# The first image's front of a non-local attention kernel: x in four loads by halves, scores ahead of the values

## The chip, the cores and the metric

The kernel runs on one core of a Trainium2 chip. The metric is the device time of one launch in microseconds (us). The core's engines are named as in the profile: PE (TensorE, the matmuls; PEld are its weight loads), DVE (VectorE), ACT (ScalarE), POOL (GpSimd) and SP (SyncE, which here only issues transfers). Each runs its own list of instructions in order, and they meet at semaphores.

## The reference

For each of four images x[b] (256 channels by 32 x 32 = 1024 pixels, fp32), with `CQK = 256 // 8 = 32`:

```
q = einsum('oc,bcn->bon', Wq, xf) + bq[None, :, None]      # 32 x 1024
k = einsum('oc,bcn->bon', Wk, xf) + bk[None, :, None]      # 32 x 1024
v = einsum('oc,bcn->bon', Wv, xf) + bv[None, :, None]      # 256 x 1024
scores = einsum('bqi,bqj->bij', q, k)                      # 1024 x 1024
attn = softmax(scores, axis=-1)
out = einsum('bcj,bij->bci', v, attn)
return out.reshape(B, Cc, W, H) + x
```

## The kernel before

Every fp32 operand is split into a high part (rounded to fp32r, names ending in `_hi`) and a low part (what is left, `_lo`), and each product is the sum of three matmuls: high by high, high by low, low by high. Making a high part is called a cut, making a low part a split. Channels lie on the partitions, so x has two tiles of 128 channels (`c` = 0, 1) of 1024 pixels, and most steps work on halves of 512 pixels (`cols(0)`, `cols(1)`).

For each image: project q and k (12 matmuls of 512 columns); project v in eight tiles of 128 pixels (six matmuls of 256 columns each, `v_tile`), which are cut and split in four pairs (`v_split` counts the pairs split); eight score tiles of 128 rows by 1024 columns (`scores`, `first_scores`; two matmuls), of which DVE takes the row maximum (`row_max`) and ACT the sum of the exponentials (`sum_exp`); then the transposed scores (`scores_t`), 16 tiles of 128 x 512, whose exponentials `w_full` are cut and split and multiplied by v (`weigh_v`: four matmuls with the high part, then two with the low part). The list of PE is written out by hand: `turn(b)` weighs image b in 16 steps, and between the steps (`FRONT`) it does the scores and projections of the next image.

The first image has no earlier image to hide behind, and has a front of its own, which the change rewrites:

- SP (line 278) loads the two channel tiles of x, 512 KB each, then the v weights `wv` (256 KB); when these have landed it loads image 1. ACT (line 485) issues the load of the small weights (`small_sb`, 66 KB: the q and k weights and biases).
- PE runs 20 matmuls on zeros (`keep_busy`) until data are there, then `first_project_qk` over the four pieces of x, channel tile by channel tile; so q and k of both halves of the pixels end within the last piece of each half.
- ACT cuts the four pieces of x, then `wv`, then makes k of both halves (`put_k_hi`), the second quarter of q (`put_q_hi`) and the full q of the second half (`put_q2_full`). DVE cuts and splits the q and k weights, splits the pieces of x, makes the first quarter of q itself (line 769), and then the low parts of q and k.
- POOL copies the weights into pairs for the later images (line 418), splits `wv` (line 424), copies two quarters of q (`put_q_dup`), splits the second half of q (`split_q2`: three instructions), then cuts and splits the first three quarters of image 1 and cuts the fourth (`cut_x1`, `split_x1`, lines 408 and 412), and then splits the weights of step 1 (`split_w(1)`, line 402), without which PE can't do the two low matmuls of step 1 (line 1015). So ten instructions lie between `wv`'s split with the q copies, and `split_w(1)`.
- PE then does v tiles 0 and 1, scores 0 to 2, v tiles 2 and 3, scores 3, v tiles 4 and 5, the turning of the four row maxima into rows (`first_rows`), v tile 6, two transposed scores, v tile 7. Step 0 (`first_weigh_v`) has score tile 4 in its middle and score tile 5 behind it, step 1 has score tile 6, and `scores_t(4)` (line 996) opens step 2.

A piece's cut is awaited at `x0_cut`, its split at `x0_split`, q and k of a half at `qk_ready`.

The scores of the first image are put into banks in which q, k and v tiles have stood or will stand: `v_tile(0, 4)` waits for `sum_exp(0, 1)`, `first_scores(3)` for `sum_exp(0, 0)`, and `first_scores(TH)` with TH = 4 for the split of two pairs of v.

Of the kernel before, what the change touches and what calls it, by code (L numbers as in the profile page):

```python
# [6 lines left out]
def nonlocal_attention(nc, x, small, wv_t, out):  # L7
# [52 lines left out]
    with ctx:  # L60
# [3 lines left out]
        def sem(name):  # L64
            return ctx.enter_context(nc.semaphore(name))
# [46 lines left out]
        x0_in = [sem(f"x0_in{c}") for c in range(CT)]  # L112
# [74 lines left out]
        def cols(h):  # L187
            return slice(h * HALF, (h + 1) * HALF)
# [4 lines left out]
        def piece(i):  # L193

            return i // 2, cols(i % 2)
# [4 lines left out]
        def q_home(i):  # L200
            return qk_home(0, i // 2)[2 * CQK:3 * CQK, quarter(i) if i < 2 else cols(0)]
# [34 lines left out]
        def qk_home(b, h):  # L236
            return slot[SLOT[QK, h] if b else h][:, 0:HALF]
# [38 lines left out]
        def _(sp):  # L276
            for c in range(CT):
                sp.dma_start(x_sb[:, 0, c, :], x_v[0, :, c, :]).then_inc(x0_in[c], DMA)
# [82 lines left out]
        def _(pool):  # L361
# [10 lines left out]
            def put_q_dup(i):  # L372
                pool.wait_ge(q_hi_put, i + 1)
                nc.gpsimd.tensor_copy(q_a[0:CQK, Q_PARTS[i]],
                                      q_a[2 * CQK:3 * CQK, Q_PARTS[i]].bitcast(fp32)).then_inc(q_dup_put, 1)
# [38 lines left out]


# [6 lines left out]
            pool.wait_ge(pair_made, 2)  # L422
            pool.wait_ge(wv_cut, 1)
# [3 lines left out]
            put_q_dup(0)  # L427
            pool.wait_ge(q_dup_put, 1)
            put_q_dup(1)
            pool.wait_ge(q_dup_put, 2)  # L430
# [53 lines left out]
        def _(act):  # L484
            act.dma_start(small_sb[:, :], small).then_inc(small_in, DMA)
            act.preload_act_table_set("natural_log_exp_and_others")
            for i in range(4):
                c, part = piece(i)
                act.wait_ge(x0_in[c], DMA)
                nc.scalar.activation(x_hi[:, 0, c, part], x_sb[:, 0, c, part], ACT.Copy).then_inc(x0_cut, 1)  # L490
# [30 lines left out]
            def first_cut_v(i):  # L521
                act.wait_ge(v_ready, i + 1)
                nc.scalar.activation(v_hi[:, 0, VT * i:VT * i + VT, :],
                                     v_home(0, i).rearrange("p (j c) -> p j c", c=C), ACT.Copy).then_inc(v_cut, 1)
# [26 lines left out]
            def put_k_hi(h):  # L551

                act.wait_ge(qk_ready, h + 1)
                nc.scalar.activation(k_a[0:2 * CQK, cols(h)], qk_home(0, h)[0:2 * CQK, :],
                                     ACT.Identity, bias=bias[0:2 * CQK, 0:1]).then_inc(k_hi_put, 1)

            def put_q_hi():

                act.wait_ge(q_lo_put, 1)
                nc.scalar.activation(q_a[2 * CQK:3 * CQK, Q_PARTS[1]], q_home(1),  # L560
                                     ACT.Identity, bias=bias[2 * CQK:3 * CQK, 0:1]).then_inc(q_hi_put, 1)
# [5 lines left out]

            act.wait_ge(wv_in, DMA)
            nc.scalar.activation(wv_hi[:, :, :], wv[:, :, :], ACT.Copy).then_inc(wv_cut, 1)
            act.wait_ge(small_in, DMA)  # L570
            put_k_hi(0)
            put_k_hi(1)
            put_q_hi()
            put_q2_full()
            first_cut_v(0)
            for t in range(TH):
                sum_exp(0, t)
            put_first_rows()
            exp(0)
# [33 lines left out]
        def _(dve):  # L613
# [5 lines left out]
            def twice(w):  # L619
# [5 lines left out]
            dve.wait_ge(wqk_cut, 1)  # L625
            nc.vector.tensor_tensor(twice(wqk_lo), wqk, twice(wqk_hi).bitcast(fp32),
                                    ALU.subtract).then_inc(wqk_split, 1)

            for i in range(4):
                c, part = piece(i)  # L630
                dve.wait_ge(x0_cut, i + 1)
                nc.vector.tensor_tensor(x_lo[:, 0, c, part], x_sb[:, 0, c, part],  # L632
                                        x_hi[:, 0, c, part].bitcast(fp32), ALU.subtract).then_inc(x0_split, 1)
# [117 lines left out]
            def finish(b, h, c):  # L751
# [9 lines left out]
                if (b, h) == (0, 0):  # L761
# [6 lines left out]
            dve.wait_ge(qk_ready, 1)  # L768
            nc.vector.tensor_scalar(out=q_a[2 * CQK:3 * CQK, Q_PARTS[0]], in0=q_home(0),
                                    scalar1=bias[2 * CQK:3 * CQK, 0:1], scalar2=None,  # L770
                                    op0=ALU.add).then_inc(q_hi_put, 1)
            put_q_lo(0)
            put_k_lo(0)
# [5 lines left out]
            split_v(0, 0)  # L779
            first_cut_v(1)  # L780
            split_v(0, 1)
            invert_sums()
            first_cut_v(2)
# [62 lines left out]
        def _(pe):  # L846
# [23 lines left out]
            def first_project_qk(i):  # L870
                c, part = piece(i)
                dst = qk_home(0, i % 2)
                if i == 0:
                    pe.wait_ge(wqk_cut, 1)
                pe.wait_ge(x0_cut, i + 1)
                nc.tensor.matmul(dst, wqk_hi[:, c, :], x_hi[:, 0, c, part], start=(c == 0), stop=False)
                if i == 0:
                    pe.wait_ge(wqk_split, 1)
                nc.tensor.matmul(dst, wqk_lo[:, c, :], x_hi[:, 0, c, part], start=False, stop=False)
                pe.wait_ge(x0_split, i + 1)  # L880
                last = nc.tensor.matmul(dst, wqk_hi[:, c, :], x_lo[:, 0, c, part], start=False, stop=(c == CT - 1))  # L881
                if c == CT - 1:
                    last.then_inc(qk_ready, 1)
# [55 lines left out]
            def v_tile(b, t):  # L939
                px = slice(t * P, (t + 1) * P)  # L940
                dst = v_home(b, t // VT)[:, t % VT * C:(t % VT + 1) * C]
                terms = [(xs[:, b % 2, c, px], w[:, c, :]) for c in range(CT)
                         for xs, w in ((x_hi, wv_hi), (x_hi, wv_lo), (x_lo, wv_hi))]
                if b == 0 and t == 0:

                    for c in range(CT):
                        for xs in (x_hi, x_lo):
                            nc.tensor.matmul(dst, xs[:, 0, c, px], wv_hi[:, c, :],
                                             start=(c == 0 and xs is x_hi), stop=False)
                    pe.wait_ge(wv_split, 1)  # L950
                    for c in range(CT):
                        nc.tensor.matmul(dst, x_hi[:, 0, c, px], wv_lo[:, c, :], start=False, stop=(c == CT - 1))
                    return
                last = group(dst, terms)
                if t % VT == VT - 1:
                    last.then_inc(v_ready, 1)

# [41 lines left out]
            def weigh_ready(b, h, j):  # L999
                if h == 0 and j % VT == 0:  # L1000
                    pe.wait_ge(v_split, 4 * b + 1 + j // VT)
                wait_w_cut(pe, PER * b + JT * h + j)
# [76 lines left out]
            keep_busy(20, QUARTER)  # L1079
            for i in range(4):  # L1080
                first_project_qk(i)
            pe.wait_ge(wv_cut, 1)
            v_tile(0, 0)
            v_tile(0, 1)
            first_scores(0)
            first_scores(1)
            first_scores(2)

            pe.wait_ge(q2_full_put, 1)
            v_tile(0, 2)  # L1090
            v_tile(0, 3)
            first_scores(3)
# [71 lines left out]
```

## Time and profile before

| | us |
|---|---|
| median of 3 runs | 164.04 (163.82 to 164.06) |
| the profiled execution, its own time | 163.81 |
| its span, first to last instruction | 162.0 |
| PE busy in the span | 157.5 (97%) |
| DVE busy | 133.9 (83%) |
| ACT busy | 109.2 (67%) |
| POOL busy | 60.0 (37%) |

Busy time counts an instruction from its start to its end, and matmuls overlap in the pipeline, so the end of one and the start of the next are read from the starts. A row of the timeline can hold several instructions in a row (x2, x4); its duration is then that of all of them.

### The profile page before, as it was taken

The numbers are of one execution on the slowest core, as the hardware profiler recorded it, in microseconds if no ns is written. First come the engines' busy times: TensorE is split into PE (matmuls) and PEld (weight loads), VectorE is DVE, ScalarE is ACT, GpSimd is POOL, SyncE is SP. The second block draws the span as 40 slices with busy tenths as digits, with TensorE's granted clock in tenths as the row PEclk, the third lists the DMA queues.
The fourth block names the chain that finished last, engine by engine and source line by source line (L and its number), as shares of the span: only waits on it lengthen the run. The fifth ranks groups of instructions, "written<-read, shape, count | busy, mean of one in ns | idle before, by whom it ended". The sixth has DMA issues, their size and how long they took to land.

```text
span 162.0 us, 2456 instructions
## 1 busy us (share of the span) xinstructions
PE 157.5 (97%) x788; PEld 132.3 (82%) x788; DVE 133.9 (83%) x215; ACT 109.2 (67%) x200; POOL 60.0 (37%) x68
## 2 busy tenths in 40 slices
PE   7999999999999999999999999999999999999993
PEld 5677887798888887798888897788888898888882
DVE  1899998888988989997989989895989779846952
ACT  3679887969999545827999646736896655756400
POOL 4479946256222316348443300342333300124500
PEclk9999999999999999999999999999999999999999
DMA  4576672152103030162711130162320330003003
GB/s 161 187 299 166 243 235 89 31 151 63 55 0 97 1 129 2 37 144 67 268 39 49 54 129 0 37 146 67 121 61 1 97 129 0 0 5 129 0 0 130
DMA packets 7780, 14.67 MB, mean 91 GB/s; under 512 B 1504, under 2 KB 2072, under 8 KB 7768
## 3 DMA queue, kind: packets, MB, share of 16 engines
q1 hardware_dynamic: 6728, 13.46, 25.4%
q0 software_dynamic: 608, 0.80, 2.2%
q10 hardware_dynamic: 432, 0.26, 0.5%
q8 instruction: 6, 0.10, 0.3%
q14 instruction: 6, 0.05, 0.1%
HBM read 4.79 MB, written 4.20 MB: 55 GB/s over the span
## 4 chain that ended last, share of the span: by engine, by line
PE 90%; DMA 2%; ACT 2%; DVE 2%; issue 1%; DVEq 0%
PE acc L1009 32%; PE acc L1015 16%; PE slot L849 11%; PE st L996 9%; PE slot L909 7%; PE slot L1009 5%; DMA small_sb<-small 2%; PE slot L1015 2%; ACT dump L504 2%; PE slot L861 2%; PE slot L866 2%; PE slot L935 1%; DVE negmax L667 1%; PE slot L881 1%; DVE x_lo L632 0%
## 5 line engine op out<-in xcount | busy, mean ns | idle before, releaser
L402 POOL TENSOR_TENSOR w_lo<-w_full,w_hi 128x512 fp32r<-128x512 f32 x21 | 28.0, 1338 | 46.6 <-ACT w_full L542 25.4
L1009 PE MATMUL acc<-w_hi,v_hi 128*128 128x512 f32 x112 | 44.3, 395 | 0.0
L1009 PE MATMUL acc<-w_hi,v_lo 128*128 128x512 f32 x112 | 44.1, 394 | 0.0
L542 ACT ACTIVATE w_full<-st 128x512 f32<-128x512 f32 x62 | 36.8, 594 | 7.6 <-PE st L996 7.5
L504 ACT ACTIVATE dump<-slot,negmax 128x1024 f32<-128x1024 f32 x29 | 32.5, 1119 | 10.5 <-DVE negmax L667 10.1
L667 DVE TENSOR_REDUCE negmax<-slot 128x1 f32<-128x1024 f32 x29 | 35.2, 1217 | 2.7 <-PE slot L909 2.7
L1015 PE MATMUL acc<-w_lo,v_hi 128*128 128x512 f32 x112 | 37.4, 396 | 0.0
L734 DVE TENSOR_TENSOR w_lo<-w_full,w_hi 128x512 fp32r<-128x512 f32 x43 | 30.7, 719 | 3.6 <-issue 0.5
L1009 PEld LDWEIGHTS acc<-w_hi,v_hi 128*128 128x128 f32 x112 | 21.1, 189 | 5.0 <-issue 0.2
L1009 PEld LDWEIGHTS acc<-w_hi,v_lo 128*128 128x128 f32 x112 | 21.2, 189 | 4.8
L1015 PEld LDWEIGHTS acc<-w_lo,v_hi 128*128 128x128 f32 x112 | 21.0, 188 | 4.8
L996 PE MATMUL st<-q_b,k_b 98*128 98x512 f32 x62 | 24.5, 398 | 0.1
L725 DVE CAST w_hi<-w_full 128x512 fp32r<-128x512 f32 x40 | 19.5, 489 | 3.0 <-ACT w_full L542 1.5
L539 ACT ACTIVATE w_hi<-st 128x512 fp32r<-128x512 f32 x24 | 14.3, 594 | 6.2 <-PE st L996 6.0
L849 PE MATMUL slot<-wv_hi,x_hi 128*128 128x256 f32 x62 | 17.4, 281 | 0.4 <-ACT dump L504 0.4
L849 PE MATMUL slot<-wv_lo,x_hi 128*128 128x256 f32 x62 | 17.4, 281 | 0.0
L849 PE MATMUL slot<-wv_hi,x_lo 128*128 128x256 f32 x62 | 17.3, 280 | 0.0
L909 PE MATMUL slot<-k_a,q_a 96*128 96x512 f32 x48 | 15.2, 397 | 0.0
L531 ACT ACTIVATE v_hi<-slot 128x512 fp32r<-128x512 f32 x12 | 7.2, 599 | 11.8 <-PE slot L849 11.8
L265 POOL DMA_DIRECT2D q_b<-shift_rows x7 | 4.2, 602 | 29.5 <-DVE shift_rows L706 27.0
L715 DVE TENSOR_TENSOR v_lo<-slot,v_hi 128x512 fp32r<-128x512 f32 x16 | 11.0, 690 | 3.8 <-ACT v_hi L531 3.7
L909 PEld LDWEIGHTS slot<-k_a,q_a 96*128 96x128 f32 x48 | 13.0, 310 | 1.1
(102 smaller groups left out, 225.2 us busy)
## 6 DMA issues: line engine op xcount, KB each, us to landing
out<-x_sb SPq DMA_DIRECT2D x7, 512.0 KB, 2.8
x_sb<-x SPq DMA_DIRECT2D x3, 1024.0 KB, 5.1
k_b<-k_a SPq DMA_DIRECT2D x8, 192.0 KB, 2.6
q_b<-q_a SPq DMA_DIRECT2D x8, 192.0 KB, 2.6
x_sb<-x SPq DMA_DIRECT2D x2, 512.0 KB, 4.2
k_a<-qk_parts SPq DMA_DIRECT2D x12, 64.0 KB, 2.0
q_a<-qk_parts SPq DMA_DIRECT2D x12, 64.0 KB, 2.2
k_a<-qk_parts POOLq DMA_DIRECT2D x6, 64.0 KB, 2.2
```

The lines of the kernel that those rows point to most:

```text
L402: nc.gpsimd.tensor_tensor(w_lo[:, r, :], w_full[:, r, :], w_hi[:, r, :].bitcast(fp32), ALU.subtract).then_inc(w_split_pool, 1)
L504: nc.scalar.activation(dump[:, t % 2, :], s_home(b, t), ACT.Exp, bias=negmax[:, t:t + 1], accum_out=rowsum[:, t:t + 1]).then_inc(rowsum_re ...
L539: nc.scalar.activation(w_hi[:, r, :], st_home(n), ACT.Exp).then_inc(w_cut_act, 1)
L542: nc.scalar.activation(w_full[:, r, :], st_home(n), ACT.Exp).then_inc(exp_done, 1)
L667: nc.vector.tensor_reduce(out=negmax[:, t:t + 1], in_=s_home(b, t), op=ALU.max, axis=AX.X, negate=True).then_inc(negmax_ready, 1)
L725: nc.vector.tensor_copy(w_hi[:, r, :], w_full[:, r, :]).then_inc(w_cut_dve, 1)
L734: nc.vector.tensor_tensor(w_lo[:, r, :], w_full[:, r, :], w_hi[:, r, :].bitcast(fp32), ALU.subtract).then_inc(w_split_dve, 1)
L849: last = nc.tensor.matmul(dst, lhs, rhs, start=(i == 0), stop=(i == len(terms) - 1))
L909: last = nc.tensor.matmul(s_home(b, t)[:, cols(h)], pixels(b, t), k_a[0:K_A, cols(h)], start=True, stop=True)
L996: nc.tensor.matmul(st_home(n), k_b[0:K_B, j * P:(j + 1) * P], q_b[0:K_B, cols(h)], start=True, stop=True).then_inc(st_ready, 1)
L1009: nc.tensor.matmul(dst, v[:, b % 2, j, c * P:(c + 1) * P], w_hi[:, n % RING, part], start=(j == 0 and v is v_hi), stop=False)
L1015: return nc.tensor.matmul(dst, v_hi[:, b % 2, j, c * P:(c + 1) * P], w_lo[:, n % RING, part], start=False, stop=(j == JT - 1))
```

## The change

It loads the first image's x in four pieces of 256 KB, both channel tiles of the first half of the pixels first, all from SP, with the small weights (now from SP too) behind the first piece. A piece `i` is now channel tile `i % 2` of half `i // 2`, so q and k of the first half are complete after two pieces. On DVE the first piece's split goes ahead of the split of the q and k weights. ACT makes k and q of the first half, then k and q of the second, then cuts `wv`; DVE no longer makes q's first quarter. POOL copies q's first quarter ahead of the weight pairs, its second behind them, and splits `wv` after that. PE runs 16 zero matmuls ahead of the projection and four behind it, and the v tiles come behind the scores; the cut of the first pair of v moves behind ACT's sums, its split on DVE behind the second pair's, and the wait counts follow.

```
@@ SP
-            for c in range(CT):
-                sp.dma_start(x_sb[:, 0, c, :], x_v[0, :, c, :]).then_inc(x0_in[c], DMA)
+            for i in range(4):
+                c, part = piece(i)
+                sp.dma_start(x_sb[:, 0, c, part], x_v[0, :, c, part]).then_inc(x0_in[i], DMA)
+                if i == 0:
+                    sp.dma_start(small_sb[:, :], small).then_inc(small_in, DMA)
             sp.dma_start(wv[:, :, :], wv_t).then_inc(wv_in, DMA)
...
-            return i // 2, cols(i % 2)
+            return i % CT, cols(i // CT)
...
@@ POOL
+            put_q_dup(0)
+            pool.wait_ge(q_dup_put, 1)
             for half, (parts, made) in enumerate(((wqk_hi, wqk_cut), (wqk_lo, wqk_split))):
...
             pool.wait_ge(pair_made, 2)
+            put_q_dup(1)
+            pool.wait_ge(q_dup_put, 2)
             pool.wait_ge(wv_cut, 1)
             nc.gpsimd.tensor_tensor(wv_lo[:, :, :], wv[:, :, :], wv_hi[:, :, :].bitcast(fp32),
...
-            put_q_dup(0)
-            pool.wait_ge(q_dup_put, 1)
-            put_q_dup(1)
-            pool.wait_ge(q_dup_put, 2)
             split_q2()
...
@@ ACT
-            act.dma_start(small_sb[:, :], small).then_inc(small_in, DMA)
...
+            act.wait_ge(small_in, DMA)
+            put_k_hi(0)
+            put_q_hi(0)
+            put_k_hi(1)
+            put_q_hi(1)
             act.wait_ge(wv_in, DMA)
             nc.scalar.activation(wv_hi[:, :, :], wv[:, :, :], ACT.Copy).then_inc(wv_cut, 1)
-            act.wait_ge(small_in, DMA)
-            put_k_hi(0)
-            put_k_hi(1)
-            put_q_hi()
             put_q2_full()
-            first_cut_v(0)
             for t in range(TH):
                 sum_exp(0, t)
             put_first_rows()
+            first_cut_v(0)
             exp(0)
...
@@ DVE
-            dve.wait_ge(wqk_cut, 1)
-            nc.vector.tensor_tensor(twice(wqk_lo), wqk, twice(wqk_hi).bitcast(fp32),
-                                    ALU.subtract).then_inc(wqk_split, 1)
             for i in range(4):
                 c, part = piece(i)
+                if i == 1:
+                    dve.wait_ge(wqk_cut, 1)
+                    nc.vector.tensor_tensor(twice(wqk_lo), wqk, twice(wqk_hi).bitcast(fp32),
+                                            ALU.subtract).then_inc(wqk_split, 1)
...
-            nc.vector.tensor_scalar(out=q_a[2 * CQK:3 * CQK, Q_PARTS[0]], in0=q_home(0),
-                                    scalar1=bias[2 * CQK:3 * CQK, 0:1], scalar2=None,
-                                    op0=ALU.add).then_inc(q_hi_put, 1)
+            put_k_lo(0)
             put_q_lo(0)
-            put_k_lo(0)
...
-            split_v(0, 0)
             first_cut_v(1)
             split_v(0, 1)
+            first_cut_v(2)
+            split_v(0, 0)
             invert_sums()
-            first_cut_v(2)
             split_v(0, 2)
...
@@ PE
+            def first_project_qk(i, w, xs):
+                c, part = piece(i)
+                return nc.tensor.matmul(qk_home(0, i // CT), w[:, c, :], xs[:, 0, c, part],
+                                        start=(c == 0 and w is wqk_hi and xs is x_hi),
+                                        stop=(c == CT - 1 and xs is x_lo))
+
+            def first_project_all():
+                pe.wait_ge(wqk_cut, 1)
+                pe.wait_ge(x0_cut, 1)
+                first_project_qk(0, wqk_hi, x_hi)
+                pe.wait_ge(x0_split, 1)
+                first_project_qk(0, wqk_hi, x_lo)
+                pe.wait_ge(x0_cut, 2)
+                first_project_qk(1, wqk_hi, x_hi)
+                pe.wait_ge(wqk_split, 1)
+                first_project_qk(0, wqk_lo, x_hi)
+                first_project_qk(1, wqk_lo, x_hi)
+                pe.wait_ge(x0_split, 2)
+                first_project_qk(1, wqk_hi, x_lo).then_inc(qk_ready, 1)
+                for i in (2, 3):
+                    pe.wait_ge(x0_cut, i + 1)
+                    first_project_qk(i, wqk_hi, x_hi)
+                    first_project_qk(i, wqk_lo, x_hi)
+                    pe.wait_ge(x0_split, i + 1)
+                    last = first_project_qk(i, wqk_hi, x_lo)
+                last.then_inc(qk_ready, 1)
...
+            def first_v_high():
+                pe.wait_ge(wv_cut, 1)
+                for c in range(CT):
+                    for xs in (x_hi, x_lo):
+                        nc.tensor.matmul(v_home(0, 0)[:, 0:C], xs[:, 0, c, 0:P], wv_hi[:, c, :],
+                                         start=(c == 0 and xs is x_hi), stop=False)
+
+            def first_v_low():
+                pe.wait_ge(wv_split, 1)
+                for c in range(CT):
+                    nc.tensor.matmul(v_home(0, 0)[:, 0:C], x_hi[:, 0, c, 0:P], wv_lo[:, c, :],
+                                     start=False, stop=(c == CT - 1))
...
-                    pe.wait_ge(v_split, 4 * b + 1 + j // VT)
+                    pe.wait_ge(v_split, 4 * b + 1 + j // VT if b + j else 2)
...
-            keep_busy(20, QUARTER)
-            for i in range(4):
-                first_project_qk(i)
-            pe.wait_ge(wv_cut, 1)
-            v_tile(0, 0)
-            v_tile(0, 1)
+            keep_busy(16, QUARTER)
+            first_project_all()
+            keep_busy(4, QUARTER)
             first_scores(0)
+            first_v_high()
             first_scores(1)
             first_scores(2)
+            first_v_low()
+            v_tile(0, 1)
             pe.wait_ge(q2_full_put, 1)
             v_tile(0, 2)
+            first_scores(3)
             v_tile(0, 3)
-            first_scores(3)
```

## Rows read from the trace of the kernel before

**Rows 1.** Busy us by stage (windows): stretch, length, PE, PEld, DVE, ACT, POOL, clock, DMA.

```profile
24.00:156.00 132.00, 132.00 (x651) 111.96 (x650) 113.00 (x181) 91.74 (x171) 43.92 (x44) 1.00 0.22 68
```

**Rows 2.** Timeline of PE: start us, us, engine, line, operation, tiles, count, [idle before].

```profile
1.06 4.45 PE L1076 MATMUL st<-idle 128*128 128x256 bf16 x20 [1.06 <-DVE idle L614]
5.27 0.59 PE L876 MATMUL slot<-x_hi,wqk_hi 128*128 128x512 f32 x1
...
8.18 0.39 PE L879 MATMUL slot<-x_hi,wqk_lo 128*128 128x512 f32 x1
8.41 0.39 PE L881 MATMUL slot<-x_lo,wqk_hi 128*128 128x512 f32 x1
...
13.69 0.74 PE L935 MATMUL acc<-k_a,q_a 96*128 96x512 f32 x2
...
22.79 0.63 PE L1015 MATMUL acc<-w_lo,v_hi 128*128 128x512 f32 x2
...
23.93 0.39 PE L996 MATMUL st<-q_b,k_b 98*128 98x512 f32 x1
```

**Rows 3.** Timeline of POOL.

```profile
5.56 0.75 POOL L418 CAST wqk_pair<-wqk_lo 128x128 fp32r<-128x128 f32 x1
7.64 1.58 POOL L424 TENSOR_TENSOR wv_lo<-wv,wv_hi 128x512 fp32r<-128x512 f32 x1 [1.34 <-ACT wv_hi L569]
...
10.72 0.61 POOL L380 CAST q_a<-qk_rest 32x512 fp32r<-32x512 f32 x1 [0.18 <-ACT qk_rest L565]
...
18.23 1.29 POOL L412 TENSOR_TENSOR x_lo<-x_sb,x_hi 128x512 fp32r<-128x512 f32 x1
19.59 1.10 POOL L408 CAST x_hi<-x_sb 128x512 fp32r<-128x512 f32 x1
20.92 1.29 POOL L402 TENSOR_TENSOR w_lo<-w_full,w_hi 128x512 fp32r<-128x512 f32 x1 [0.23 <-ACT w_full L542]
```

**Rows 4.** Timeline of SP's queue, the transfers that it issues.

```profile
0.74 0.86 SPq L278 DMA_DIRECT2D x_sb<-x  x2
...
6.45 0.39 SPq L282 DMA_DIRECT2D x_sb<-x  x1
```

**Rows 5.** Windows of the first loads; last columns: DMA share and GB/s.

```profile
1.75:2.75 1.00, 1.00 (x7) 0.69 (x6) 0.00 (x0) 0.71 (x1) 0.94 (x2) 1.00 0.62 133
2.75:4.10 1.35, 1.35 (x8) 0.98 (x7) 0.00 (x0) 0.00 (x0) 0.09 (x1) 1.00 1.04 401
...
5.25:5.75 0.50, 0.50 (x4) 0.45 (x2) 0.50 (x2) 0.40 (x1) 0.50 (x2) 1.00 1.02 397
```

**Rows 6.** Timeline of ACT.

```profile
4.50 1.15 ACT L490 ACTIVATE x_hi<-x_sb 128x512 fp32r<-128x512 f32 x2 [2.04 <-DMA x_sb<-x]
...
6.88 0.62 ACT L569 ACTIVATE wv_hi<-wv 128x512 fp32r<-128x512 f32 x1
8.21 1.31 ACT L554 ACTIVATE k_a<-slot,small_sb 64x512 fp32r<-64x512 f32 x2 [0.72 <-PE slot L881]
9.55 0.47 ACT L560 ACTIVATE q_a<-slot,small_sb 32x256 fp32r<-32x256 f32 x1
```

**Rows 7.** Timeline of DVE.

```profile
4.71 0.29 DVE L624 CAST wqk_hi<-small_sb 128x256 fp32r<-128x256 f32 x1 [3.43 <-DMA small_sb<-small]
...
5.38 2.68 DVE L632 TENSOR_TENSOR x_lo<-x_sb,x_hi 128x512 fp32r<-128x512 f32 x4
...
14.57 1.22 DVE L667 TENSOR_REDUCE negmax<-acc 128x1 f32<-128x1024 f32 x1
...
19.53 0.68 DVE L734 TENSOR_TENSOR w_lo<-w_full,w_hi 128x512 fp32r<-128x512 f32 x1
```

**Rows 8.** Chain that ended last, in order of time: start us, us, what.

```profile
18.42 0.71 PE slot L849 x6
```

**Rows 9.** Timeline of POOL and of DVE, 48 to 51 us.

```profile
48.43 1.30 POOL L402 TENSOR_TENSOR w_lo<-w_full,w_hi 128x512 fp32r<-128x512 f32 x1 [2.96 <-issue]
49.34 0.93 DVE L734 TENSOR_TENSOR w_lo<-w_full,w_hi 128x512 fp32r<-128x512 f32 x1
```

More of the change, by code:

```diff
@@ L110, in nonlocal_attention @@
         slot = [ctx.enter_context(nc.psum_tensor(f"slot{i}", [P, N], fp32)) for i in range(2)]
-        x0_in = [sem(f"x0_in{c}") for c in range(CT)]
+        x0_in = [sem(f"x0_in{i}") for i in range(4)]
         x1_in = sem("x1_in")
@@ L488, in _ @@
                 c, part = piece(i)
-                act.wait_ge(x0_in[c], DMA)
+                act.wait_ge(x0_in[i], DMA)
                 nc.scalar.activation(x_hi[:, 0, c, part], x_sb[:, 0, c, part], ACT.Copy).then_inc(x0_cut, 1)
@@ L555, in put_k_hi, with put_q_hi @@
                                      ACT.Identity, bias=bias[0:2 * CQK, 0:1]).then_inc(k_hi_put, 1)
-            def put_q_hi():
-                act.wait_ge(q_lo_put, 1)
-                nc.scalar.activation(q_a[2 * CQK:3 * CQK, Q_PARTS[1]], q_home(1),
+            def put_q_hi(i):
+                if i:
+                    act.wait_ge(q_lo_put, i)
+                nc.scalar.activation(q_a[2 * CQK:3 * CQK, Q_PARTS[i]], q_home(i),
                                      ACT.Identity, bias=bias[2 * CQK:3 * CQK, 0:1]).then_inc(q_hi_put, 1)
@@ L766, in finish @@
                                                scalar=bv_sb[:, c:c + 1], in1=x_sb[:, b, c, cols(h)], op0=ALU.add, op1=ALU.add).then_inc(acc_read, 1)
-            dve.wait_ge(qk_ready, 1)
-            nc.vector.tensor_scalar(out=q_a[2 * CQK:3 * CQK, Q_PARTS[0]], in0=q_home(0),
-                                    scalar1=bias[2 * CQK:3 * CQK, 0:1], scalar2=None,
-                                    op0=ALU.add).then_inc(q_hi_put, 1)
+            put_k_lo(0)
             put_q_lo(0)
-            put_k_lo(0)
             put_k_lo(1)
@@ L868, in project_qk @@
                 both_halves(CT - 1).then_inc(qk_ready, 1)
-            def first_project_qk(i):
+            def first_project_qk(i, w, xs):
                 c, part = piece(i)
[L872 to L883, printed above, removed]
+                return nc.tensor.matmul(qk_home(0, i // CT), w[:, c, :], xs[:, 0, c, part],
[21 more added lines that the diff above has]
+                last.then_inc(qk_ready, 1)
             def pixels(b, t):
@@ L943, in v_tile @@
                          for xs, w in ((x_hi, wv_hi), (x_hi, wv_lo), (x_lo, wv_hi))]
[L944 to L953, printed above, removed]
                 last = group(dst, terms)
```

## The prediction

> **What bounds the kernel now.** I read the table of busy time by stage first. From 24 to 156 us PE is busy for 132.00 of 132.00 us [rows 1]. So nothing behind 24 us can be won by ordering, and whatever the change gains is the shift of the moment at which PE takes up that unbroken run. I measure it at `scores_t(4)`, line 996, which starts at 23.93 [rows 2]. Before that point the reader looks, engine by engine in the timeline, for what releases PE last. The last place where it can be held is step 1: its two low matmuls, line 1015, start at 22.79 [rows 2] and need `split_w(1)` of POOL, which ran from 20.92 to 22.21 [rows 3]: 0.58 us to spare. Behind them come two matmuls of score tile 6; a matmul of 512 columns takes 0.23 (8.18 to 8.41), so 22.79 + 4 x 0.23 = 23.72, and the 0.21 up to 23.93 is a wait, for the sums of tile 4.
>
> POOL matters because it has no slack of its own: from `split_q2` at 10.72 to the cut that ends at 20.69 its ten instructions follow one another [rows 3]. It then waited 0.2 for its operand. Whatever shifts 10.72 shifts all of it.
>
> A difference of 0.2%, 0.33 us, is about what a measurement of this kernel tells from no change.
>
> **Loads.** Before, two loads of 512 KB were issued in 0.86 us from 0.74 on [rows 4], the small one from ACT at the same time. 133 GB/s moved up to 2.75, 401 behind [rows 5]. Both (592 KB) were through at 2.75 + (592 - 133) / 401 = 3.89; ACT started on x at 4.50 [rows 6], 0.61 later, DVE on the weights at 4.71 [rows 7], 0.82 later. After, 262 KB end at 2.75 + 129 / 401 = 3.07 and the small load, 68 KB, at 3.24. With the same lags ACT starts at 3.68 and DVE at 4.06. The bounds: the small load lags no more than x did (3.85), or nothing is won (4.71). I take 4.06, since the order in the queue is what the change turns. SP issues three loads more, at 0.43 each 1.3 us; this hides behind the transfers, of which each piece needs 0.65 at 401 GB/s. `wv` has the same bytes ahead of it, so it still lands at about 6.45, when image 1 is issued [rows 4], and ACT asks for it later than that.
>
> A page of the Trainium skill speaks against the cutting: "DMA: Bandwidth & Descriptors", section "Rules for kernel authors", wants 1 MiB or more in a transfer. Here the 256 KB of `wv` moved at 397 GB/s [rows 5] beside 401 in the window before, so by the row the four pieces cost nothing; by the rule the pieces would land later than I say, which is the fourth rival below.
>
> **Projection.** DVE's chain of weight cut, weight split and four splits of x took 4.71 to 8.06 [rows 7], 3.35 us; with the same instructions it ends at 4.06 + 3.35 = 7.41. PE: twenty matmuls of 256 columns on zeros took 4.45, one starting every 0.21 [rows 2], which is the 1.2 GHz level (the clock column shows 1.00 throughout, and doesn't tell it); 512 columns in 0.23 are 2.4 GHz. Sixteen end at 1.06 + 16 x 0.21 = 4.47. The first piece is cut at 3.68 + 0.62 = 4.30, so PE goes on without a gap: high by high 4.47, high by low behind the first split (4.39 + 0.7) at 5.1, both at the low level, until 5.53. With the clock up at about 5.5 as before (the matmul at 5.27 took 0.59, later ones 0.39), ten are left: the last starts at 5.53 + 9 x 0.23 = 7.63 and ends at 8.02. Before, the last ended at 8.41 + 0.39 = 8.80. So q and k are whole 0.78 earlier.
>
> **The cut of wv, and what hangs on it.** It was done at 6.88 + 0.62 = 7.50 [rows 6], ahead of k. Now it stands behind k and q of both halves: k of half 1 starts at 8.02 + 0.1 (before, half 0 ended at 8.41 - 3 x 0.23 + 0.39 = 8.11 and ACT began at 8.21), the step to the next is 0.63 (two took 1.31, one of them 0.68), q 0.45, the cut 0.62: done at 9.80. POOL follows 0.14 later as before (7.50 to 7.64) and needs 1.29, as its other subtractions of this size do, or 1.58 as it took before beside DVE's splits [rows 3]; at 9.9 DVE reads PSUM, so I take 1.29: `wv_lo` ends at E = 11.23 (to 11.52). The weight pairs (0.75 the longer) fit between the two q copies, since POOL has until 9.94; without that cover they would add to E. `split_q2` follows at E + 0.07 = 11.30, against 10.72: POOL is **0.58 later** (to 0.87).
>
> **PE's side.** Behind E stand two low matmuls of v tile 0 and tiles 1 and 2, 14 matmuls at 0.117 (six in 0.71 [rows 8]): score tile 3 starts at 11.23 + 0.06 + 1.64 = 12.93 and is whole 0.7 later (two in 0.74 [rows 2]); the fourth row maximum starts at 13.65, against 14.57 [rows 7]: **0.92 earlier**. What follows it (row maxima to rows, exponentials, the first weighing) has the same instructions on its path; ACT's added cut of v pair 0 fits into its wait for the transposed scores. DVE's three earlier row maxima start from about 10.0 and don't hold it. PE would reach line 1015 at 22.79 - 0.92 = 21.87.
>
> **The sum.** POOL doesn't let it. Its cut chain ends 0.58 later: `split_w(1)` runs from 20.76 + 0.58 = 21.34 to 22.63, PE starts its low matmuls at 22.69, four matmuls later stands at 23.62, against 23.93: -0.31. (The wait for the sums of tile 4 is gone, they come 0.9 earlier.) With 1.58 for `wv_lo` it is -0.02; with 3.85 for DVE's start little more, since PE's zero matmuls end at 4.47 anyhow. Later consumers have room: image 1 is split by POOL's last piece at 28 us plus the same 0.6, and image 2's load goes out 0.6 later, for work far behind. Against its own execution that is 163.81 - 0.31 = 163.50; that execution lies 0.23 under the median, so I say 164.04 - 0.31 = **163.7** for the median. Its own range is 163.4 to 164.0, from POOL's instructions each stretched or shortened by a collision.
>
> **Rivals.**
> 1. *POOL gains back what it lost.* Before, its cut at 19.59 took 1.10 instead of 0.61 (10.72), because DVE's `split_w(0)` had started at 19.53 [rows 3, 7]. If DVE meets a gap or waits itself, POOL has 0.49 less: -0.8, 163.2. For it: the two move apart by 1.5 us. Against: POOL has no gap there, so they meet again.
> 2. *DVE loses the meeting, and it gets slower.* At 49.34 DVE's split started while POOL's (48.43 to 49.73) ran, and ended at 50.27, 0.54 behind it [rows 9]: the one that came second waited whole. `split_w(0)` asks at 19.53 - 0.92 = 18.61. POOL's subtraction of 18.23 then stands at 18.81 to 20.10. If DVE comes 0.2 later than I think, it waits for 20.10 and ends at 20.64, against 20.21; its row maximum of tile 4, the sums and score tile 6 follow as much later: +0.43, 164.5. It decides at 18.81. The Trainium skill has this as a rule ("SBUF — State Buffer", section "Who interferes with whom": GpSimd and a VectorE instruction with two SBUF inputs exclude each other for a whole instruction, and the one that issues first wins); the rows agree.
> 3. *The clock stays low.* Between 4.9 and 5.1 PE now idles, and it waits for pieces. If the low level lasts through the projection, ten matmuls cost 0.2 more each: E comes 2 us later, +1.7, 165.7. For it: before, PE had no gap from 1.06 to the rise. Against: the gap is 0.2 us.
> 4. *The loads win nothing.* Then DVE starts at 4.71 as before and its chain ends at 8.06, PE at 8.5 instead of 8.02: E + 0.47, +0.16, 164.2. Against it: the bytes ahead of the first piece are halved.
>
> **Chances.** Forecast 0.52, half of it beyond -0.33; rival 1 0.15, rival 2 0.15, rival 3 0.08, rival 4 0.10. Faster 0.26 + 0.15 = 0.41; within 0.2% 0.26 + 0.10 = 0.36; slower 0.23. The range goes from 163.0, a little under rival 1, to 164.8, above rival 2; it leaves out rival 3 and little else.
>
> **What would show it.** First x cut at about 3.7 and weight cut at 4.1; the last projection matmul ending near 8.0; `wv_hi` done at 9.8; `wv_lo` ending near 11.2; the fourth row maximum at 13.7; `split_w(1)` ending at 22.6 and PE's low matmuls of step 1 idle before it by about 0.8. I am wrong if PE is not held by POOL there, if projection matmuls start 0.43 apart behind 6 us, or if `split_w(0)` takes over 1 us.

## The result, and the profile after

After takes **165.82 us** (165.12 to 166.88) against 163.96 (163.8 to 164.2) on the same chip: ratio 1.0116 [1.0083, 1.0150], **slower by 1.2%**. I had said 163.7, with 163.0 to 164.8 as the range. The profiled execution of after took 165.12 (span 163.3), the lowest of the timed ones; that of before 163.81 (span 162.0).

**Where the loss stands.** Stage windows and PE's timeline:

```profile
24.00:156.00 132.00, 132.00 (x649) 111.85 (x649) 113.51 (x182) 93.03 (x174) 43.91 (x44) 1.00 0.23 73
```

```profile
6.12 0.50 PE L872 MATMUL slot<-x_hi,wqk_hi 128*128 128x512 f32 x1 [0.70 <-ACT x_hi L492]
...
8.35 0.42 PE L872 MATMUL slot<-x_lo,wqk_hi 128*128 128x512 f32 x1
...
13.91 0.62 PE L947 MATMUL acc<-k_a,q_a 96*128 96x512 f32 x2
...
21.58 0.73 PE L1031 MATMUL acc<-w_lo,v_hi 128*128 128x512 f32 x2 [0.27 <-DVE w_lo L738]
...
24.06 0.63 PE L1031 MATMUL acc<-w_lo,v_hi 128*128 128x512 f32 x2
...
25.25 0.40 PE L1011 MATMUL st<-q_b,k_b 98*128 98x512 f32 x1
```

PE is again unbroken from 24 to 156 [rows 1], and `scores_t(4)` starts at 25.25 instead of 23.93 [rows 2]: 1.32 later, which is the difference of the executions (165.12 - 163.81 = 1.31). The place that I measured at was right, and the sign was wrong. (The median is 0.7 above this execution; what adds that is shown by the experiments.) The last projection matmul starts at 8.35 against 8.41, and score tile 3 at 13.91 against 13.69 [rows 2], so the front won nothing. The fourth row maximum starts at 14.58 against 14.57; in this execution the loss arises behind it.

**What holds PE there.** The chain that ended last, in order of time (start us, us, what):

```profile
10.33 0.50 PE acc L947
...
14.58 1.24 DVE negmax L671
...
15.91 0.98 DVE shift_parts L678
...
20.26 1.27 DVE w_lo L738
...
21.58 0.73 PE acc L1031 x2
```

It runs over DVE and not over POOL. DVE's timeline and POOL's:

```profile
6.10 2.12 DVE L636 TENSOR_TENSOR x_lo<-x_sb,x_hi 128x512 fp32r<-128x512 f32 x3 [0.90 <-ACT x_hi L492]
...
14.58 1.23 DVE L671 TENSOR_REDUCE negmax<-acc 128x1 f32<-128x1024 f32 x1 [0.22 <-PE acc L947]
15.91 0.97 DVE L678 CAST shift_parts<-negmax 128x4 fp32r<-128x4 f32 x1
...
20.18 1.35 DVE L738 TENSOR_TENSOR w_lo<-w_full,w_hi 128x512 fp32r<-128x512 f32 x1
```

```profile
10.81 1.29 POOL L431 TENSOR_TENSOR wv_lo<-wv,wv_hi 128x512 fp32r<-128x512 f32 x1 [0.28 <-ACT wv_hi L577]
12.16 0.61 POOL L383 CAST q_a<-qk_rest 32x512 fp32r<-32x512 f32 x1
...
15.57 1.29 POOL L415 TENSOR_TENSOR x_lo<-x_sb,x_hi 128x512 fp32r<-128x512 f32 x1
...
19.69 1.28 POOL L415 TENSOR_TENSOR x_lo<-x_sb,x_hi 128x512 fp32r<-128x512 f32 x1
...
22.08 1.30 POOL L405 TENSOR_TENSOR w_lo<-w_full,w_hi 128x512 fp32r<-128x512 f32 x1
```

Before, in the timelines of both engines, the same cast of four columns fell into the end of another instruction of POOL, a cut up to 16.08, and the small subtraction behind the cast was 0.02 ahead of POOL's next subtraction:

```profile
15.47 0.61 POOL L408 CAST x_hi<-x_sb 128x512 fp32r<-128x512 f32 x1
15.90 0.20 DVE L674 CAST shift_parts<-negmax 128x4 fp32r<-128x4 f32 x1
16.14 0.17 DVE L676 TENSOR_TENSOR shift_parts<-negmax,shift_parts 128x4 fp32r<-128x4 f32 x1
16.16 1.31 POOL L412 TENSOR_TENSOR x_lo<-x_sb,x_hi 128x512 fp32r<-128x512 f32 x1
```

DVE arrives there at the same time in both kernels (15.90, 15.91). POOL's chain of cuts and subtractions is 12.16 - 10.72 = 1.44 later [rows 3], so another of its instructions stands there: a subtraction from 15.57 to 16.86, and the cast ends at 16.88. It costs 0.97 - 0.20 = 0.77. Before, the good meeting was luck, by 0.02 us. `split_w(0)` starts at 20.18, inside the subtraction of 19.69 to 20.97, and ends 0.56 behind it: 1.35 against 0.68 [rows 7], 0.67 more. The two make 0.77 + 0.67 = 1.44 (the same figure as POOL's shift by chance), of which 0.13 is won back between them. The second ends at 21.53, 1.32 behind 19.53 + 0.68 = 20.21, and PE waits for it. `split_w(1)`, which I had taken for the bound, ends at 23.38, ahead of PE's low matmuls at 24.06.

**Loads.** SP's queue, ACT's timeline and the windows (last columns: DMA share, GB/s):

```profile
1.19 0.42 SPq L281 DMA_DIRECT2D small_sb<-small  x1
1.65 1.38 SPq L279 DMA_DIRECT2D x_sb<-x  x3
```

```profile
3.50 0.63 ACT L492 ACTIVATE x_hi<-x_sb 128x512 fp32r<-128x512 f32 x1 [1.47 <-DMA x_sb<-x]
5.44 2.05 ACT L492 ACTIVATE x_hi<-x_sb 128x512 fp32r<-128x512 f32 x3 [1.30 <-DMA x_sb<-x]
10.03 0.63 ACT L577 ACTIVATE wv_hi<-wv 128x512 fp32r<-128x512 f32 x1
```

```profile
1.75:2.75 1.00, 1.00 (x7) 0.69 (x6) 0.00 (x0) 0.28 (x1) 0.94 (x2) 1.00 0.85 280
2.75:4.10 1.35, 1.35 (x8) 0.98 (x7) 0.29 (x1) 0.60 (x1) 0.09 (x1) 1.00 0.88 225
4.10:5.25 1.15, 1.15 (x5) 0.59 (x3) 1.03 (x2) 0.03 (x1) 0.00 (x0) 1.00 0.88 292
```

The first piece is cut at 3.50, before the 4.50 of [rows 6]. Up to 2.75 more moves than before (280 GB/s against 133). But behind it, where 401 GB/s moved [rows 5], it is 225 and 292, the second piece is cut at 5.44 only, and DVE (0.90) and PE (0.70) wait.

### The profile page after: what moved, and what is told of

Its sections match the earlier page's. It is cut to its first block, busy times and chain, and to the rows that moved or that the text cites. A ratio compares the mean times of both kernels' runs of the same rounds, so it can differ in the third digit from the quotient of the medians.

```text
span 163.3 us, 2458 instructions
## 1 busy us (share of the span) xinstructions
PE 157.3 (96%) x788; PEld 131.7 (81%) x788; DVE 135.1 (83%) x214; ACT 110.1 (67%) x201; POOL 59.0 (36%) x68
## 4 chain that ended last, share of the span: by engine, by line
PE 88%; DVE 7%; DMA 2%; SPq 0%; issue 0%; ACT 0%; DVEq 0%
PE acc L1025 31%; PE acc L1031 16%; PE slot L849 11%; PE st L1011 9%; PE slot L921 7%; PE slot L1025 5%; PE slot L1031 2%; DMA x_sb<-x 2%; PE slot L861 2%; PE slot L866 2%; PE slot L947 1%; DVE x_lo L636 1%; DVE v_lo L719 1%; DVE k_a L646 1%; DVE w_lo L738 1%; DVE negmax L671 1%
## 5 line engine op out<-in xcount | busy, mean ns | idle before, releaser
L738 DVE TENSOR_TENSOR w_lo<-w_full,w_hi 128x512 fp32r<-128x512 f32 x43 | 31.4, 734 | 3.3
```

What stands on the lines that cost most here:

```text
L738: nc.vector.tensor_tensor(w_lo[:, r, :], w_full[:, r, :], w_hi[:, r, :].bitcast(fp32), ALU.subtract).then_inc(w_split_dve, 1)
```

## The experiments

**A** is the meetings of DVE with POOL's subtractions, **B** the loads: they land late and differently each time. In its first form B blames the small load in SP's queue, in its second the halves (rows of 2 KB instead of 4).

**after_again**: after, unchanged.

> The changed kernel once more, for a second profile. Theory A (DVE waits for POOL): in its first profile DVE's first shift cast took 0.97 us instead of 0.20 and split_w(0) 1.35 instead of 0.68, together 1.44 us, about the whole of the 1.3 by which that execution was longer; a second profile shows the same two, within 0.3. Theory B (loads): the loads by halves move at 225 to 307 GB/s instead of 400, the second piece is there at 5.4 instead of my 4.3, and as this differs from execution to execution it makes the spread of 1.8 us; the second profile has the second piece elsewhere (4.5 to 6.5) and its length moves with it.

165.78 (165.56 to 166.41), ratio 1.0128 [1.0104, 1.0152]; profiled execution 165.70. Its timelines of ACT and DVE:

```profile
6.78 1.28 ACT L492 ACTIVATE x_hi<-x_sb 128x512 fp32r<-128x512 f32 x2 [1.01 <-DMA x_sb<-x]
...
16.47 0.99 DVE L678 CAST shift_parts<-negmax 128x4 fp32r<-128x4 f32 x1
...
20.77 1.35 DVE L738 TENSOR_TENSOR w_lo<-w_full,w_hi 128x512 fp32r<-128x512 f32 x1
```

Both meetings stand though everything is 0.6 later: POOL hangs on the same late loads, so the two keep their phase. Here the second piece is cut at 5.14, the third at 6.78 only. Both causes are seen.

**loads_only** (of before: the four half loads and the small one behind the first, nothing else) and **order_only** (of after: the loads of before).

```
loads_only, in before:
-            for c in range(CT):
-                sp.dma_start(x_sb[:, 0, c, :], x_v[0, :, c, :]).then_inc(x0_in[c], DMA)
+            for i in range(4):
+                c, part = piece(i)
+                sp.dma_start(x_sb[:, 0, c, part], x_v[0, :, c, part]).then_inc(x0_in[i], DMA)
+                if i == 0:
+                    sp.dma_start(small_sb[:, :], small).then_inc(small_in, DMA)
...
-            act.dma_start(small_sb[:, :], small).then_inc(small_in, DMA)
...
order_only, in after: the same lines the other way round
```

> The kernel before with the loads alone changed: four by halves from SP, the small one behind the first, in the order of the change; everything else as before. Theory A expects no change beyond 0.3 us, since the order of POOL and DVE is that of before. Theory B expects the last pieces later than the 5.8 of before (6 to 6.5), the last projection matmul later by as much, so 0.3 to 0.8 us more, and a spread over 0.8 us.

> The changed kernel with the loads of before: two of 512 KB from SP, the small one from ACT. Theory A expects the two long DVE instructions to stay, and 165.0 to 165.5. Theory B expects the spread to fall to that of before (0.4 us), the second piece at 5.85 as before, and the time near the lower end of the changed kernel's, 165.1 or less.

loads_only: 165.14 (165.1 to 165.21), 1.0079 [1.0064, 1.0094]. order_only: 166.77 (165.52 to 166.92), 1.0162 [1.0125, 1.0199]; three of its four executions take 166.7 to 166.9, one 165.52. Both halves of the change lose by themselves, and each loses more than either theory had put down (0.8 at most for loads_only, 165.5 at most for order_only). loads_only, timelines of POOL and DVE:

```profile
16.30 1.27 POOL L415 TENSOR_TENSOR x_lo<-x_sb,x_hi 128x512 fp32r<-128x512 f32 x1
...
14.93 1.22 DVE L669 TENSOR_REDUCE negmax<-acc 128x1 f32<-128x1024 f32 x1
...
16.46 1.13 DVE L678 TENSOR_TENSOR shift_parts<-negmax,shift_parts 128x4 fp32r<-128x4 f32 x1
```

DVE is 14.93 - 14.57 = 0.36 later, and that is enough: its subtraction of the shift, 0.02 ahead of POOL's before, now starts inside POOL's and takes 1.13 instead of 0.17. 0.36 + 0.96 = 1.32, the measured 1.3. So A needs no new order, only a change of phase. order_only, PE's timeline:

```profile
5.34 0.77 PE L870 MATMUL slot<-x_hi,wqk_hi 128*128 128x512 f32 x1 [0.69 <-ACT x_hi L490]
...
8.86 0.63 PE L870 MATMUL slot<-x_hi,wqk_lo 128*128 128x512 f32 x1
9.29 0.54 PE L870 MATMUL slot<-x_lo,wqk_hi 128*128 128x512 f32 x1
```

With x at the old time, PE's sixteen zero matmuls end 0.69 too early, and the projection's start 0.43 apart, the 1.2 GHz step, until 9.3: the low clock of my third rival.

**order_busy20**: order_only with twenty zero matmuls.

```
-            keep_busy(16, QUARTER)
+            keep_busy(20, QUARTER)
```

> The run with the loads of before and the order of the change (166.77, projection matmuls 0.43 apart up to 9.3 us), with twenty zero matmuls ahead of the projection again instead of sixteen. Theory C (the gap between the zero matmuls and the first piece, 4.7 to 5.3, kept TensorE at its low level) expects matmuls 0.23 apart behind about 6.5 us, 1.2 to 1.6 us less (165.2 to 165.6) and a spread under 0.4. Rival: the order of the projection with its waits keeps the clock low by itself; then 166.5 or more.

165.50 (165.41 to 165.56), 1.0100 [1.0086, 1.0114]: 1.27 less than order_only. Its timeline of PE, where the step is 0.23 from the second row on:

```profile
1.06 3.70 PE L1090 MATMUL st<-idle 128*128 128x256 bf16 x20 [1.06 <-DVE idle L616]
...
7.52 0.40 PE L870 MATMUL slot<-x_hi,wqk_hi 128*128 128x512 f32 x1
7.75 0.40 PE L870 MATMUL slot<-x_hi,wqk_lo 128*128 128x512 f32 x1
```

So the low clock is what cost order_only that. That the gap kept it low isn't shown. Twenty zero matmuls took 3.70, where order_only's sixteen took 3.60: the last six start 0.11 apart, the 2.4 GHz step, from 3.94 on, ahead of the four that were added and at a time when order_only still went at 0.21; and 0.47 without work follows them here too. Only the times speak for the four: all of order_busy20's executions lie at 165.4 to 165.6, one in four of order_only's. Cast (0.97) and `split_w(0)` (1.35) stay, and with them the loss.

**small_act**: after, the small load from ACT again. **whole_sp**: before, the small load on SP behind the first 512 KB. **small_first**: before, on SP ahead of x.

```
small_act, in after:
-                if i == 0:
-                    sp.dma_start(small_sb[:, :], small).then_inc(small_in, DMA)
...
+            act.dma_start(small_sb[:, :], small).then_inc(small_in, DMA)
whole_sp, in before (small_first: the SP line ahead of the loop):
+                if c == 0:
+                    sp.dma_start(small_sb[:, :], small).then_inc(small_in, DMA)
...
-            act.dma_start(small_sb[:, :], small).then_inc(small_in, DMA)
```

> The changed kernel with the small load from ACT again, x still in four loads from SP. If it is the small load's place in SP's queue that holds the second piece, this lands at 4.3 to 4.7 and the time falls by 0.5 to 0.9 us (theory B, first form). If it is the halves themselves that are slow (second form), the second piece stays at 5.2 or later and the time stays within 0.4 of the changed kernel's. Theory A expects no change but that of chance meetings.

> The kernel before with one edit: the small load issued by SP behind the first 512 KB of x, not by ACT. If the small load's place in SP's queue slows what is behind it (form 1), the windows behind 2.75 us move less than 320 GB/s and the second tile of x lands at 6.3 or later, with a spread over 0.5 us. If it is the halves (form 2), the windows stay near 400 GB/s; the small load then lands about 0.2 later than before and the time stays within 0.4 of before.

> The kernel before with the small load ahead of x in SP's queue. The weights are cut at about 3.6 instead of 4.71, and DVE has their split behind it when x comes, so its chain ends up to 0.4 earlier. As POOL's chain hangs on the same projection, both shift together: 163.4 to 163.8, if x isn't later by as much. If the small load slows what is behind it, x lands later and the time is 164.0 or more.

small_act: 165.17 (165.11 to 165.23), 1.0081 [1.0066, 1.0096], 0.65 less than after and without its spread. The difference is one of medians: the profiled executions of the two take 165.13 and 165.12, after's being its fastest. whole_sp: 164.64 (164.43 to 165.88), 1.0059 [1.0036, 1.0082]. small_first: 163.73 (163.59 to 165.07), 1.0001 [0.9986, 1.0017]. Windows of small_act, and behind them of whole_sp, of a later stretch:

```profile
1.75:2.75 1.00, 1.00 (x7) 0.67 (x6) 0.00 (x0) 0.71 (x1) 0.94 (x2) 1.00 0.66 171
2.75:4.10 1.35, 1.35 (x8) 0.95 (x7) 0.04 (x1) 0.21 (x1) 0.09 (x1) 1.00 1.07 362
4.10:5.25 1.15, 1.14 (x4) 0.36 (x2) 0.96 (x3) 1.01 (x2) 0.00 (x0) 1.00 0.92 306
```

```profile
5.25:5.75 0.50, 0.50 (x4) 0.40 (x3) 0.50 (x2) 0.00 (x0) 0.48 (x1) 1.00 0.63 225
...
6.25:6.75 0.50, 0.50 (x3) 0.40 (x2) 0.03 (x1) 0.00 (x0) 0.00 (x0) 1.00 0.20 78
```

Halves without the small load among them move at 362 and 306, where after has 225 and 292; but after is ahead by then (280 against 171), and summed over 1.75 to 5.25 the two have moved 1012 and 920 KB, before 1143.

The other traces put most of this on the halves. The six kernels with halves and the small load from ACT (small_act, clear_small, mend1 to mend4) moved 917 to 1012 KB in that stretch, the four with it behind the first piece (after, after_again, loads_only, clear_after) 833 to 920, those with whole tiles and it from ACT (before, order_only, order_busy20, clear_before) 1130 to 1144. small_act is the best of its six: in clear_small, with the same loads, the third piece comes late as well; timeline of ACT:

```profile
6.39 1.29 ACT L495 ACTIVATE x_hi<-x_sb 128x512 fp32r<-128x512 f32 x2 [0.87 <-DMA x_sb<-x]
```

Whole tiles with the small load among them trail off: in before the loads fill the DMA engines up to 5.75 [rows 5] and are through; in whole_sp the share falls from 0.63 to 0.20, and ACT cuts the second tile at 7.12 instead of 5.82 (timelines of both). This is whole_sp's slowest execution, 165.88, the others take 164.4 to 164.8; and in it DVE's subtraction of the shift waits for POOL (1.28), so a meeting is part of its loss. Cut or whole, the kernels with the small load in SP's queue behind the first piece are the slower ones, B's first form; in what the queue moves, the second form holds too. The issue of the small load itself puts the next piece 0.46 later (1.65 instead of 1.19 in SP's queue above), and how much of the 0.65 that is, no run separates.

In small_act three pieces are cut without a gap from 3.89 on, yet its projection ends no earlier; timeline of PE:

```profile
5.89 0.63 PE L871 MATMUL slot<-x_hi,wqk_hi 128*128 128x512 f32 x1
6.32 0.85 PE L871 MATMUL slot<-x_hi,wqk_lo 128*128 128x512 f32 x2
...
8.39 0.39 PE L871 MATMUL slot<-x_lo,wqk_hi 128*128 128x512 f32 x1
```

From 5.89 to 6.32 is 0.43, the low level, and so is the step inside the pair at 6.32; the step is 0.23 from 7.00 on, before from 6.55. Earlier data was worked on at the lower clock.

**clear_after** and **clear_before**: POOL's subtractions of image 1's first three quarters cut to one column, in after and in before (the rest of that low part is left out). **clear_small**: clear_after with small_act's load.

```
+            nc.gpsimd.memset(x_lo[:, 1, :, 0:3 * QUARTER].bitcast(fp32), 0.0).then_inc(x1_zero, 1)
...
-                nc.gpsimd.tensor_tensor(x_lo[:, 1, :, quarter(i)], x_sb[:, 1, :, quarter(i)],
-                                        x_hi[:, 1, :, quarter(i)].bitcast(fp32), ALU.subtract).then_inc(x1_split, 1)
+                part = quarter(i) if i == 3 else slice(i * QUARTER, i * QUARTER + 1)
+                nc.gpsimd.tensor_tensor(x_lo[:, 1, :, part], x_sb[:, 1, :, part],
+                                        x_hi[:, 1, :, part].bitcast(fp32), ALU.subtract).then_inc(x1_split, 1)
```

> The changed kernel with POOL's three subtractions for the low part of image 1's first three quarters cut to one column each (the rest is set to zero early, so that low part is left out). DVE then meets no POOL instruction of 1.3 us. Theory A (DVE waits for POOL) expects the first shift cast at 0.2 instead of 0.97, split_w(0) at 0.7 instead of 1.35, and 1.2 to 1.5 us less than the changed kernel: 164.0 to 164.5. Theory B (the loads are the loss) expects 165.3 or more, since the loads stay.

> The same cut in the kernel before, as control. There the shift cast takes 0.20 and split_w(0) 0.68 already, so theory A expects 163.6 to 163.9, no change; if POOL's load as such slowed PE or DVE (rival), this would gain as much as clear_after, over 1 us.

> Both suspected costs taken away from the changed kernel: the small load from ACT, and POOL's three subtractions for image 1 cut to one column each (that low part is left out). If the two are the whole loss and add up, 165.8 - 0.6 - 1.35 = 163.85, within 0.3 of the kernel before. If something else of the change costs too, it stays above 164.2; if the front had a gain hidden behind the two, it comes out under 163.5.

clear_after: 164.44 (163.83 to 165.6), 1.0040 [1.0021, 1.0060], 1.38 less than after. clear_before: 163.80 (163.66 to 163.93), 0.9993 [0.9984, 1.0002]: the cut alone gives nothing. clear_small: 163.86 (163.6 to 164.2), 0.9999 [0.9990, 1.0008]. Timeline of DVE in clear_after:

```profile
16.24 0.56 DVE L682 CAST shift_parts<-negmax 128x4 fp32r<-128x4 f32 x1
...
20.09 0.68 DVE L742 TENSOR_TENSOR w_lo<-w_full,w_hi 128x512 fp32r<-128x512 f32 x1
```

The cast still waits for POOL's cut there (0.56), `split_w(0)` for nothing. So the meetings cost after 1.38 and the small load's place 0.65 (165.82 - 165.17), 2.03 together; after is 1.86 over before in its own comparison, 1.96 (165.78 - 163.82) in that of after_again, and with both away the change neither gains nor loses. Each costs about as much with the other away: 1.31 (165.17 - 163.86) and 0.58 (164.44 - 163.86). Taken alone, after against small_act isn't clear of after's spread; after_again (0.61) and the 0.58 are. The two causes account for the whole loss.

**mend1 to mend4**: small_act with POOL's work put elsewhere, to miss the meetings and keep the computation whole.

```
mend1, POOL's order as it is then (other waits left out):
             cut_x1(0)
             pool.wait_ge(shift_ready, 1)
             split_x1(0)
...
             cut_x1(1)
             pool.wait_ge(w_split_dve, SPLIT_COUNT[0])
             cut_x1(2)
             split_w(1)
             split_x1(1)
             split_w(3)
             split_x1(2)
             cut_x1(3)
             split_x1(3)
mend2: also PE's first_scores(3) ahead of v_tile(0, 2)
mend3: mend2; POOL has split_x1(1) ahead of cut_x1(2), without the wait for
       step 0's split, and split_x1(2), cut_x1(3) ahead of split_w(3)
mend4: mend3; DVE has split_v(0, 2) ahead of split_v(0, 0), and the wait
       counts follow
```

> Whole computation: the changed kernel with the small load from ACT, and POOL's work for image 1 put where DVE doesn't need the way: it waits for the shifts before its first subtraction, for split_w(0) before its third cut, does split_w(1) then, and the rest of image 1 after it. Theory A expects both long DVE instructions gone and 1.2 to 1.4 us less than with the small load from ACT alone (165.17): 163.7 to 164.0, level with the kernel before. Theory B expects 165.0.

> mend1 with score tile 3 ahead of v tile 2, so that the fourth row maximum needn't wait for it (0.20 to 0.28 us idle before it in the changed kernel). Theory A: another 0.2 to 0.3 less, 163.4 to 163.7, faster than the kernel before by 0.2 to 0.5. Rival: the fourth row maximum starts 0.3 earlier, but PE then waits for split_w(1) of POOL, and nothing is won over mend1.

> mend2 with another order on POOL: it waits for the shifts before its first subtraction, splits two quarters of image 1 and cuts the third, does split_w(1), then the third subtraction and the fourth cut, and only the last subtraction behind split_w(3), as in the kernel before. Theory A (what counts is which DVE instruction meets which POOL instruction) expects the shift cast and sub at 0.2 each, split_w(0) at no more than 0.9, no DVE instruction over 1.2 us up to 32 us, and 163.5 to 164.0. If what mend1 lost late came not from the moved subtractions but from the front itself, it stays at 164.8.

> mend3, whole computation, with DVE's split of v pair 0 behind that of pair 2, since in mend3 DVE stood idle 0.57 us for ACT's moved cut of that pair. If that idle time is what mend3 still lost, split_w(0) starts at about 19.3 instead of 19.78 and the time is 163.8 to 164.0, level with the kernel before; if not, it stays at 164.3.

mend1: 164.80 (164.63 to 165.16), 1.0057 [1.0044, 1.0069]. mend2: 165.09 (164.89 to 165.29), 1.0072 [1.0059, 1.0084]. mend3: 164.34 (164.25 to 164.4), 1.0031 [1.0019, 1.0044]. mend4: 164.23 (163.66 to 164.48), 1.0018 [1.0007, 1.0028]. All four missed the time that I expected; mend4 came out where I had put it if DVE's idle time was not what mend3 lost (164.3). mend1 misses the early meetings: `scores_t(4)` at 24.02, 0.09 behind before. But the moved subtractions meet DVE later; timelines of DVE and POOL:

```profile
26.54 1.60 DVE L738 TENSOR_TENSOR w_lo<-w_full,w_hi 128x512 fp32r<-128x512 f32 x1
...
26.12 1.47 POOL L413 TENSOR_TENSOR x_lo<-x_sb,x_hi 128x512 fp32r<-128x512 f32 x1
```

In mend2 and mend3 DVE idles 0.54 and 0.57 for ACT's cut of v pair 0, which the change had put behind the sums. In mend4 that wait is gone, and `split_w(0)` comes at 19.62, 0.03 behind POOL's cut of 19.59; timelines of DVE and POOL:

```profile
19.62 1.12 DVE L736 TENSOR_TENSOR w_lo<-w_full,w_hi 128x512 fp32r<-128x512 f32 x1 [0.20 <-ACT w_full L542]
...
19.59 0.61 POOL L409 CAST x_hi<-x_sb 128x512 fp32r<-128x512 f32 x1
```

By their medians, none of the four beats before.

## Why the prediction was wrong, point by point

- **Where to measure** was right: PE unbroken behind 24, and `scores_t(4)` gives the whole difference.
- **Loads** failed behind the first piece. First piece 3.50 (I said 3.68) and weights 3.68 (4.06) were near. I had 133 GB/s up to 2.75 and 401 behind it; it was 280, then 225 and 292. `wv` was there a microsecond later than I said (image 1 is issued at 7.48, not at 6.45), which cost nothing, since ACT asked for it at 10.03. The Trainium skill, "DMA: Bandwidth & Descriptors", section "Rules for kernel authors", had spoken against cutting x; in what was moved the traces agree (917 to 1012 KB with halves, 1130 to 1144 with whole tiles), and my "by the row the four pieces cost nothing" was wrong. In the time the cutting isn't seen, for clear_small has the halves and takes what before takes; what the median loses is 0.65, by the small load's place. The same page, section "Issuing engines are not separate DMA queues", says that another issuing engine saves only the time of issuing; small_act and after, which differ in that alone, differ by 0.65, of which issuing can be 0.46; what is left over isn't clear of the spread, so these runs don't contradict the page. Whether the queue does more stays open: the traces show the rates, not why.
- **Projection.** I had the last matmul start at 7.63. It was 8.35: the second piece was late. Without that lateness (small_act) it was 8.39, because the low clock lasted longer than to my 5.5. Both eat the 0.78 that I had counted; rivals 3 and 4, each in part. That rival 3's time, 165.7, lies near the measured 165.82 is chance: in after's profile the step is 0.23 from 6.45 on, and the loss came by another way. (Two sums were off by a little, 1.06 + 16 x 0.21 is 4.42 and not 4.47, 5.53 + 9 x 0.23 is 7.60; neither matters here.)
- **The cut of wv** was mis-sized by the same: 10.66 instead of 9.80, and `wv_lo` ends at 12.10 instead of 11.23.
- **PE's side** failed in "0.92 earlier": the fourth row maximum starts at 14.58, before 14.57. 0.72 of the 0.93 missing came with the projection (8.35 instead of 7.63). The rest is a path: I let all of it hang on `wv_lo`, but the chain goes through DVE's low parts of k, which I didn't walk: the second matmul of the first score, at 10.33, waits for `put_k_lo(1)`. PE's low matmuls of v tile 0 start at 12.22, 0.12 behind `wv_lo`, when score tile 2 is issued.
- **"What follows it has the same instructions on its path"** is the step that gave the wrong sign. From the fourth row maximum to the end of `split_w(0)` it took 20.21 - 14.57 = 5.64 before and 21.53 - 14.58 = 6.95 after: the same instructions, two of them held by POOL. With the row maximum 0.01 later, that is the whole 1.32 of the profiled executions. I had put one of the two down as rival 2, at 0.15 and +0.43; it took 0.67. I had looked at DVE's wide subtractions only, and not seen the cast of four columns, whose wait costs as much.
- **"POOL doesn't let it"**: POOL was 1.44 later, not 0.58, but not the bound: `split_w(1)` ended at 23.38, ahead of the matmuls that need it. What its shift did was to turn its phase against DVE's.

Two of my three signs of being wrong came: PE was not held by POOL there, and `split_w(0)` took over 1 us.

Shown by experiments: the meetings (clear_after against clear_before), and that the small load's place costs time (clear_small against clear_after, small_act against after_again). Not shown: what in SP's queue makes the loads late, and what decided in order_only and order_busy20 when the clock rose. Only read from timelines: why mend1 to mend4 don't reach before.

## What to carry to other kernels

Where GpSimd and VectorE both work from SBUF on a chain without slack, lay their timelines over each other before and after every shift, small instructions included: in loads_only a shift of 0.36 us cost 1.3. When a chain is moved, forecast the phase of the two chains, and not only their lengths. And walk the new chain through every engine: the one that bound before isn't the one that binds after.

## What the hardware showed that I had not expected

- A cast of 128 x 4 on DVE waits like a wide one: 0.97 instead of 0.20 behind POOL's subtraction. The Trainium skill ("SBUF — State Buffer", section "Who interferes with whom") has it that a port pair which GpSimd and VectorE share is held by one of them for a whole instruction; the runs agree. POOL's one-input cut holds DVE too (mend4: 1.12 instead of 0.68).
- x in four loads of 256 KB moved less than in two of 512 KB: 917 to 1012 KB from 1.75 to 5.25 us, against 1130 to 1144, with the small load from ACT in both. 66 KB in SP's queue behind the first piece left 833 to 920; in one execution with whole tiles the last tile was cut at 7.12 in place of 5.82. Ahead of all of x (small_first) it did no harm to the time.
- In kernels that all begin with the same sixteen zero matmuls, PE left the 1.2 GHz step at 9.3 us (order_only), at 6.74 (small_act) and at 3.94 (order_busy20, ahead of its four added ones). The runs don't show what decides it.
